# A causal mask that ScalarE writes into the scores' bank, in place of two mask matmuls a step

## The reference

```python
q = rms_norm((x @ wq).reshape(B, L, 16, 128), q_norm_w)      # x is layer-normed first
k = rms_norm((x @ wk)..., k_norm_w); k_ctx = rms_norm((ctx @ wk_ctx)..., k_norm_w)
q, k = rope(q), rope(k)
k_full, v_full = concat([k_ctx, k]), concat([v_ctx, v])
mask = concat([zeros(L, T), where(j > i, -inf, 0)])
probs = softmax(einsum(q, k_full) / sqrt(128) + mask)
x = x + tanh(g_xattn) * (einsum(probs, v_full) @ wo)
x = x + tanh(g_ffn) * ffn(layernorm(x))     # gate, up (256 to 768), down, weights rounded to fp8 values
```

## Time and profile before

| | us |
|---|---|
| median of 3 runs | 325.38 (325.27 to 327.22) |
| the profiled execution | 325.29 |
| its span in the trace | 323.4 |
| TensorE busy | 297.3 (92%) |
| ScalarE busy | 231.9 (72%) |
| VectorE busy | 227.0 (70%) |
| GpSimd busy | 182.6 (56%) |

### The profile page before, as it was taken

The page is one execution under the profiler, slowest core; times in us unless marked ns, Lnnn a source line. Parts: engine busy times, 40 slices in busy tenths (PEclk is TensorE's granted clock), DMA queues, the critical chain, the costliest instruction groups (busy, mean ns, idle before and its releaser), DMA issues.

```text
span 323.4 us, 6512 instructions
## 1 busy us (share of the span) xinstructions
PE 297.3 (92%) x2212; PEld 233.8 (72%) x2212; DVE 227.0 (70%) x477; ACT 231.9 (72%) x892; POOL 182.6 (56%) x178
## 2 busy tenths in 40 slices
PE   3777998996999999999999999999999999998866
PEld 1333566663777778888887888788878888777764
DVE  1357899889676688759987777658774765576454
ACT  2266687864687889897898768887887778776522
POOL 1154587566964467556874586456755685465320
PEclk9999899998999999999999999999999999999999
DMA  6999000000000010000100010000000000000001
GB/s 194 392 390 352 3 16 2 0 1 0 19 0 3 1 32 3 2 0 2 34 2 0 2 33 2 2 1 10 9 3 0 2 17 3 0 2 16 2 1 34
DMA packets 6721, 12.84 MB, mean 40 GB/s; under 512 B 801, under 2 KB 4257, under 8 KB 6689
## 3 DMA queue, kind: packets, MB, share of 16 engines
q1 hardware_dynamic: 6400, 12.00, 10.3%
q10 hardware_dynamic: 288, 0.43, 0.6%
HBM read 11.38 MB, written 1.05 MB: 38 GB/s over the span
## 4 chain that ended last, share of the span: by engine, by line
PE 57%; DVE 16%; ACT 13%; issue 6%; POOL 4%; DMA 3%; ACTq 0%; DVEq 0%; POOLq 0%
PE ps_kv L392 7%; PE ps_scores L615 6%; PE ps_attn L655 5%; PE ps_y L434 5%; PE ps_y L439 5%; PE ps_transposed L412 5%; PE ps_q L392 4%; ACT probs L851 4%; PE ps_probs L412 4%; PE ps_ff L482 4%; PE ps_q L400 3%; ACT squares L684 3%; PE ps_ff L502 3%; DMA const<-in_constants_dram 2%; PE ps_kv L400 2%
## 5 line engine op out<-in xcount | busy, mean ns | idle before, releaser
L851 ACT ACTIVATE probs<-ps_scores,exp_bias,q_scale 128x128 f32<-128x128 f32 x128 | 56.8, 456 | 15.8 <-DVE exp_bias L1125 15.8
L1253 POOL TENSOR_TENSOR q_rot<-q_rot,q_sin 128x512 f32<-128x512 f32 x32 | 41.5, 1298 | 22.2 <-DVE q_sin L977 22.0
L1298 POOL TENSOR_TENSOR probs<-probs,row_inv 128x512 f32<-128x512 f32 x32 | 36.8, 1149 | 20.0 <-DVE row_inv L1185 19.9
L1204 POOL TENSOR_TENSOR q_scale<-ssq_eps,minus_half 128x4 f32<-128x4 f32 x32 | 38.4, 1199 | 10.3 <-DVE ssq_eps L1156 10.2
L1215 POOL TENSOR_TENSOR fuse_lo<-fuse,fuse_hi 128x256 fp32r<-128x256 f32 x21 | 15.4, 732 | 45.0 <-ACT fuse_hi L693 45.0
L684 ACT ACTIVATE squares<-ps_q 128x128 bf16<-128x128 f32 x128 | 33.9, 289 | 9.2 <-PE ps_q L392 3.3
L827 ACT ACTIVATE pt<-ps_probs 128x512 f32<-128x512 f32 x32 | 19.1, 598 | 22.6 <-PE ps_probs L412 22.6
L615 PE MATMUL ps_scores<-kt,qt 128*64 128x128 f32 x512 | 34.4, 279 | 0.0
L655 PE MATMUL ps_attn<-pt,values 128*128 128x256 f32 x128 | 33.4, 383 | 0.0
L615 PEld LDWEIGHTS ps_scores<-kt,qt 128*64 128x64 f32 x512 | 30.1, 141 | 0.0
L973 DVE TENSOR_TENSOR q_rot<-ps_q,rope 128x512 f32<-128x512 f32 x32 | 21.9, 686 | 11.2 <-ACT squares L684 11.2
(11 more groups left out here) (148 smaller groups left out, 873.5 us busy)
## 6 DMA issues: line engine op xcount, KB each, us to landing
q_raw<-in_wq_dram SPq DMA_DIRECT2D x4, 512.0 KB, 9.1
o_raw<-in_wo_dram SPq DMA_DIRECT2D x4, 512.0 KB, 10.6
ctx_t<-in_ctx_dram SPq DMA_DIRECT2D x8, 128.0 KB, 2.6
out_dram<-x_sb SPq DMA_DIRECT2D x8, 128.0 KB, 1.7
stage<-in_gate_w_dram SPq DMA_DIRECT2D x2, 384.0 KB, 10.7
stage<-in_up_w_dram SPq DMA_DIRECT2D x2, 384.0 KB, 11.7
x_sb<-in_x_dram SPq DMA_DIRECT2D x1, 768.0 KB, 13.6
stage<-in_down_w_dram SPq DMA_DIRECT2D x2, 384.0 KB, 11.6
```

The source lines that it names most:

```text
L851: last = nc.scalar.activation(probs[:, i, :], ps_s[:, i * P:(i + 1) * P], ACT.Exp, bias=exp_bias[:, i:i + 1], scale=q_scale[:, k % 2, i:i ...
L1204: return nc.gpsimd.tensor_tensor(dst, src, minus_half[:, 0:src.shape[1]], ALU.pow)
L1253: nc.gpsimd.tensor_tensor(q_rot[:, :, :], q_rot[:, :, :], q_sin[:, :, :], ALU.add)\
L1298: nc.gpsimd.tensor_tensor(probs[:, :, :], probs[:, :, :], row_inv[:, :].unsqueeze(2).broadcast_to([P, 4, P]), ALU.mult).then_inc(probs_rea ...
```

## The change

The mask of all 128 keys (zero for the context's) stands ready as float32 in the table of constants, [128, 128] in place of [128, 64]. ScalarE copies it, broadcast over the four heads, into `ps_s` with one activation: for step 0 as soon as the table is in, for every later step right behind the exponentials of the step before, which are the last that read the bank. The two mask matmuls are gone, and the first score matmul waits for `mask_set`. All score matmuls add (`start=False`). One matmul of ones at the very start (`open_scores`) writes the whole bank once, for which the tile of ones is 512 wide. VectorE's casts of mask and identity are gone.

```diff
-C_COS, C_SIN, C_MASK, C_ID, C_ALL = 0, DIM, 2 * DIM, 2 * DIM + LEN, 2 * DIM + LEN + P
+C_COS, C_SIN, C_MASK, C_ID, C_ALL = 0, DIM, 2 * DIM, 2 * DIM + P, 2 * DIM + 2 * P
...
-        mask = sb("mask", [P, LEN], bf16)
-        ident_bf = sb("ident_bf", [P, P], bf16)
+        mask = const[:, C_MASK:C_MASK + P]
...
-        ones_bf = sb("ones_bf", [P, P], bf16)
+        ones_bf = sb("ones_bf", [P, 512], bf16)
...
 # TensorE, one_step
-                    if isinstance(u, int) and step(u, k) == 0:
-                        pe.wait_ge(tables_ready, 6)
+                    pe.wait_ge(mask_set, step(u, k) + 1)
                     scores = four(ps_s)
-                    for r in range(2):
-                        rows = slice(r * LEN, (r + 1) * LEN)
-                        nc.tensor.matmul(scores[rows, :, rows], ident_bf[:, rows],
-                                         mask[:, :].unsqueeze(1).broadcast_to([P, HPG, LEN]),
-                                         start=True, stop=False, skip_group_check=True)
                     for h in range(HPG):
...
+            def open_scores():
+
+                pe.wait_ge(ones_set, 1)
+                nc.tensor.matmul(ps_s[:, :], ones_bf[:, 0:P], ones_bf[:, :], start=True, stop=True,
+                                 skip_group_check=True).then_inc(scores_open, 1)
+
+            open_scores()
             run_steps(pe, one_step)
...
 # ScalarE
+            def set_mask(s):
+
+                if s == 0:
+                    act.wait_ge(const_in, 16)
+                    act.wait_ge(scores_open, 1)
+                else:
+                    act.wait_ge(exp_ready, s)
+                nc.scalar.activation(four(ps_s), mask.unsqueeze(1).broadcast_to([P, HPG, P]), ACT.Copy)\
+                    .then_inc(mask_set, 1)
...
                     last.then_inc(exp_ready, 1)
+                if is_step(u, k + 1):
+                    set_mask(step(u, k + 1))
...
 # VectorE, tables()
                 dve.wait_ge(const_in, 16)
-                nc.vector.tensor_copy(mask[:, :], const[:, C_MASK:C_MASK + LEN]).then_inc(tables_ready, 1)
-                dve.wait_ge(ident_in, 16)
-                nc.vector.tensor_copy(ident_bf[:, :], ident).then_inc(tables_ready, 1)
```

More of the change, by code:

```diff
@@ L199, in build @@
         half_set = sem("half_set")
+        scores_open, mask_set = sem("scores_open"), sem("mask_set")
         tables_ready = sem("tables_ready")
@@ L457, in spread_nan @@
                     for i in range(WIDE):
-                        last = nc.tensor.matmul(ps_f[:, 0:1], ones_bf[:, :], ff_bad[:, i:i + 1], start=(i == 0),
+                        last = nc.tensor.matmul(ps_f[:, 0:1], ones_bf[:, 0:P], ff_bad[:, i:i + 1], start=(i == 0),
                                                 stop=(i == WIDE - 1))
@@ L1356, in shape_constants @@
     late = np.arange(LEN)[None, :] > np.arange(LEN)[:, None]
-    table[:, C_MASK:C_MASK + LEN] = np.tile(np.where(late, MASKED, 0.0), (2, 1))
+    for r in range(2):
+        rows = slice(r * LEN, (r + 1) * LEN)
+        table[rows, C_MASK:C_MASK + P][:, rows] = np.where(late, MASKED, 0.0)
     table[:, C_ID:C_ID + P] = np.eye(P)
```

## The result

The changed kernel takes **334.15 us** (median of 4 runs, 333.36 to 334.99), the kernel before 325.45 us beside it: a ratio of 1.0242 [1.0201, 1.0282], 2.4% slower. The prediction said slower, 331.5 us with a range of 327.5 to 334.8; the time lies inside, at its upper end. The profiled executions are both from the lower heap: spans of 331.6 and 323.4 us, 8.2 us apart. The sum had said 6.1.

What follows compares the result with a forecast made beforehand. It took the late steps to be bound by a round through ScalarE, VectorE and TensorE. Mask delays +8.1 and removed matmuls -2.0 gave +6.1 on 325.29 us, 331.4; with the median 0.1 above, 331.5 us, range 327.5 to 334.8.

Steps and rivals of the forecast that it cites:

- The mechanism: On ScalarE behind each step's last exponential: the mask delays what follows where ScalarE goes on without a pause, 0.63 us.
- two ways that carry a delay on: Late steps: through `ot_lo` to the output projection; from a tile's first step also through squares, VectorE, rotation, row maximum, bias.
- The masks are hidden: Rival: idle ScalarE time absorbs the masks and TensorE loses 4.2 us of work: 321.2 us, chance 5%.
- Only the old chain is lengthened: Rival: only masks on the chain of before cost, 5.6 us less 2.8 for scores: +2.8, 328.2 us, chance 15%.
- TensorE's clock falls in late tiles: Rival: longer ScalarE rounds cause three more clock falls, 1.7 us lost in each: 336.5 us, chance 6%.
- The price of a mask: On ScalarE behind the exponentials: 0.12 + 0.03 + 0.48 = 0.63 us per unpaused step, bounds 0.46 to 0.75.
- The number of masks on the path: 17 masks in steps 12 to 30 reach the end; with step 4 they add 8.1 us.
- The mask matmuls: Removed pair on TensorE saves 0.13 us a step in about 15 steps: -2.0 us, bounds 1.5 and 4.8.
- Steps 0 to 11: Nearly no delay reaches the end, only step 4 adds 0.05; these steps up to 1 us shorter together.
- The late stretches: Mask delays of 1.61 us in steps 12 to 15, 2.15 in 16 to 19, 1.56 in 20 to 23, 2.76 in 24 to 30.
- The start: Two VectorE casts save 0.25 us, larger table taken as costing 0.25: together nothing, bounds -0.25 and +1.25.
- What would show it: Signs expected in the profile after: mask row and spacing, waits, ScalarE's chain share, mask's line count, lengths of steps.

Runs made afterwards that it cites:

- Experiment 1: Kernel before, mask matmuls kept, plus a spare ScalarE copy of the mask's shape, never read, behind each step's exponentials: 335.19 us, ratio 1.0287.
- experiments 3 and 4: ScalarE writes the mask in steps 0 to 11 alone (326.5 us, 1.0008) or in steps 12 to 31 alone (334.41 us, 1.0263), matmuls in the others.
- experiment 5: The changed kernel with the mask one place later on ScalarE, behind `qt`, so `ot_hi` starts as early as before: 330.64 us, ratio 1.0150.
- experiment 2: Kernel before without its two mask matmuls and nothing in their place, so attention is unmasked: 324.26 us, ratio 0.9956.
- experiment 6: The changed kernel with a mask activation of 256 columns in place of 512: 328.87 us, ratio 1.0096.
- experiment 4: ScalarE writes the mask for steps 12 to 31 alone, matmuls write it in steps 0 to 11: 334.41 us, ratio 1.0263.
- the last experiment: ScalarE masks steps 0 to 11; VectorE later, mostly behind `ot_lo`, from step 29 behind the row sums' reciprocal: 325.32 us, ratio 0.9971.
- experiment 8: ScalarE masks steps 0 to 11; VectorE later, behind `ot_lo`, or behind the reciprocal for a tile's third step: 325.74 us, ratio 1.0002.
- experiments 7 to 9: ScalarE masks steps 0 to 11, VectorE masks from step 12, in three placements: 326.35, 325.74 and 325.32 us.

## Why the prediction was right, and where its sizes were off

**The mechanism** was right: idle ScalarE time of 91 us did not help, because the mask sits behind the last exponential, where ScalarE doesn't pause in most steps. Experiment 1 shows it without any mask, experiments 3 and 4 by the steps; experiment 5 shows that the place counts, for 2.5 of the 7.6 us. Of the two ways that carry a delay on, I had put the one over `ot_lo` and the output projection first and called the one over the squares a second. In the changed kernel's chain it is the other way round: the output projection stands in it once behind step 12, and all other late steps go over the squares or along VectorE's own order.

**The rivals.** *The masks are hidden* (321.2 us) fell with the result, and by experiment 2 that time could not have been reached with any placement: no mask at all is 324.26. *Only the old chain is lengthened* (328.2): it fell too. Every late stretch is lengthened by more than 1 us, steps 16 to 20 by 2.30, where that rival had two whole masks and a piece of a third. *TensorE's clock falls in late tiles*: the granted clock's row of the kernel after has one dip, around 80 us, and none behind it, though the chain leaves TensorE for far longer.

**The price of a mask**: 0.69 us where I had 0.63. The step that failed took 0.48 from start to start from copies that read PSUM and write SBUF. In the other direction an activation is as long, but the next starts 0.54 behind. The line through the copies of 256 and 1,024 columns, which I worked out as 0.51 and set aside, was nearer. By the Trainium skill ("ScalarE: Activation LUTs", *What ACT_TABLE_LOAD costs*) the estimate was 0.52; the trace has 0.54. The rule of the Trainium skill ("ScalarE: Activation LUTs", *Step-by-step: what each stage is for*) that ScalarE's writes to the bank are the faster ones holds for the activation itself, 602 ns in the changed kernel against 631 in experiment 1, and changes nothing for the time, since the next one starts 0.54 behind in both.

**The number of masks on the path**: 17 were counted, experiment 6 gives 16.7. With the price of 0.69 my terms would have come to 8.1 + 17 x 0.06 = 9.1. Experiment 1, which has nothing else in it, is 7.83 us longer late than before. So 17 x 0.69 less 7.8, 3.9 us, is taken up by pauses, where my terms had 2.6; experiment 6 gives 3.8 (17 x 0.47 less the 3.92 that it is longer, and 0.24 for the matmuls), which is no second proof, since the 17 comes from it. Too small a price and too small a cushion hid each other. Which of the pauses are the longer ones I did not follow up.

**The mask matmuls**: the step that failed worst. I gave them 15 x 0.13 = 2.0 us, half of it in steps 0 to 11. A pair is worth 0.08, as the first of the float32 matmuls takes longer than it did behind the pair. From the last matmul ahead of the mask or the scores to the first behind them it is 1.31 us before and 1.23 after in most steps, and 1.23 in experiment 2 too. Experiment 2 gives 0.41 early and 0.47 late, 0.9 together, for removing all of them. And where the path is on ScalarE and VectorE, as in the changed kernel, there is less to gain: 0.24 late.

**Steps 0 to 11**: "nearly none", and together up to 1 us shorter; measured 0.73 longer. That is 1.7 us of the miss, the largest term. From one step's exponentials to the next one's, after minus before: +0.62 from 11 to 12, the one mask of experiment 4; +0.18 from 3 to 5, where I had 0.05, and where the chain of waits holds the masks behind steps 3 and 4; -0.19 from 7 to 11, where the removed pairs would give 0.39 by experiment 2 and the masks cost half of it; +0.14 from 6 to 7, which experiment 4 has as well (+0.16) with before's instructions there, so it is not the masks. The gain of eight pairs, 1.0 us, did not come. I had looked at the wait of ScalarE as the cushion, and not at the way over VectorE next to it with 0.12 us of room.

**The late stretches**: the forecast at the same points was +1.5, +2.0, +1.4, +1.3 and +1.2, less 0.26 for the two pairs that had no place, 7.2; measured were +1.06, +2.30, +1.69, +1.48 and +1.06, 7.6. **The start** was within 0.2 us: the exponentials of step 0 begin at 26.98 and began at 27.15. Kernels without a fall of the clock ahead of that point have it anywhere from 26.67 to 27.37, so that the casts and the larger table cancelled is likely and not shown.

**The number** lies in the range in part by luck. The range comes mainly from the price (-2.9 to +2.0 us on 17 masks), and the prediction doesn't say how its other bounds were added. The largest miss, 1.7 us in steps 0 to 11, had no bound of its own there.

**What would show it**, point by point: 32 activations of 0.60 us: yes. The next 0.48 behind: no, 0.54. 0.03 behind the read: yes. The output projection waits for `ot_lo`: yes, the two rows above. The chain's share of ScalarE at 17%: no, 37%, as the round stays on ScalarE and VectorE through nearly all late steps. The mask's line a dozen times or more: 23 times. Steps 16 to 19 longer by 2.0 us: 2.30. Steps 0 to 11 shorter: no. No wait of TensorE for the mask: right.

## What to carry to other kernels

An engine's idle time is worth something only at the point of its order where the new instruction stands: read there, for each turn of the loop, how long the engine waits and which wait ends last behind it, also on the ways through other engines. Then price both sides before anything is written: take the old instruction away alone and add the new one alone, with its result unused. Here the first gave a ceiling of 0.4% and the second a loss of 7.8 us in the late steps, 2.9% in all with its longer fall of the clock, which settles the change; and of two free engines the one that was idle at the right places (VectorE behind `ot_lo`) reached that ceiling.

## What the runs showed of the hardware that I had not expected

**The start-to-start time of activations depends on what they read.** Copies of 512 columns that read the matmuls' banks: 0.48 to 0.49 us, as `ot_hi` to `qt` above. Copies of 512 columns out of SBUF behind the wait for the accumulator's read: 0.54 us, whether they write to a bank (602 ns each) or to SBUF (631 ns). Out of SBUF right behind another copy, in experiment 5: 0.52. With 256 columns out of SBUF into a bank: 0.32 us, 388 ns each. The duration of one does not tell it.

**TensorE's clock at the start is not the same in each execution.** The times of each kernel lie in two heaps some 1.5 us apart: before 325.3 to 325.5 and 327.2, after 333.4 and 334.9, the last experiment 324.4 to 324.6 and 326.0 to 326.5. The profiled executions show what differs. Busy us of the engines in stretches of 4 us and, third from the end, TensorE's granted clock, of the kernel after and then of experiment 8:

```profile
20.00:24.00 4.00, 2.24 (x11) 1.49 (x12) 1.46 (x4) 3.77 (x12) 2.11 (x2) 1.00 1.07 376
24.00:28.00 4.00, 3.92 (x24) 1.81 (x22) 1.91 (x4) 3.18 (x16) 0.00 (x0) 1.00 1.03 408
```

```profile
20.00:24.00 4.00, 2.26 (x10) 1.53 (x11) 1.33 (x4) 3.59 (x11) 1.98 (x2) 0.83 1.07 375
24.00:28.00 4.00, 4.00 (x22) 1.94 (x22) 0.38 (x1) 2.21 (x11) 0.00 (x0) 0.75 1.03 411
```

The two kernels are the same up to there, and TensorE was as busy in both (2.24 and 2.26 of 4 us). The clock falls to half (1.2 GHz) for a part of the time in one execution and not in the other. (0.17 + 0.25) x 4 us = 1.7 us of work are lost, and step 0's exponentials begin at 28.54 instead of 26.98. The three profiled executions with such a fall ahead of step 0 (experiments 7 to 9) lie in their kernels' upper heaps; the six from lower heaps (before, after, experiments 2 and 4 to 6) have none. What such a fall costs depends on where it comes. The kernel before has one a little later, from 30.98 to 34.40 us, which the changed kernel doesn't have:

```profile
28.00:32.00 4.00, 2.06 (x8) 1.21 (x8) 3.93 (x7) 2.29 (x14) 3.32 (x3) 0.87 0.87 329
32.00:36.00 4.00, 4.00 (x28) 2.33 (x28) 2.85 (x6) 1.72 (x13) 2.28 (x2) 0.70 0.01 4
```

It too is 1.7 us of work, and nothing is lost by it: from the exponentials of step 0 to those of step 1 it is 10.71 us, and 10.70 in the changed kernel, where TensorE is busy for only 2.71 of the 4 us from 32 to 36 and so has pauses to spare. So it does not distort the comparison of the two. The fall behind the pause at 76 us is there in all, but in the spare copy's kernel it held for longer:

```profile
76.00:80.00 4.00, 0.87 (x6) 0.57 (x8) 3.96 (x8) 1.04 (x8) 1.72 (x1) 0.76 0.00 0
80.00:84.00 4.00, 4.00 (x26) 3.40 (x23) 3.68 (x7) 2.49 (x11) 3.74 (x3) 0.50 0.02 4
84.00:88.00 4.00, 4.00 (x24) 2.69 (x23) 2.60 (x7) 2.98 (x10) 3.86 (x4) 0.89 0.01 2
```

Means of 0.76, 0.50 and 0.89 are 3.4 us of work, against 1.7 in the earlier trace rows. The kernel with ScalarE's masks in steps 0 to 11 has the same longer fall, and in both the step behind it, 6 to 7, takes 11.2 us where the others take 9.9 to 10.6. This is a part of why the spare copy's kernel measured 335.19 us, though its late stretches are those of the changed kernel. What decides whether the clock falls stays open. For reading such small changes it means that one profiled execution can be off by more than the effect. The stretches behind step 12, where no trace has a fall of the clock before step 31's exponentials and which repeat within 0.05 us between kernels of the same order, can't be off by that much.
